# A macaron block on one core: ramp steps moved in front of GpSimd's tile work, and one more split on ScalarE

## The reference

```python
x = x + 0.5 * ffn(layernorm(x))      # 8 experts, one per token (argmax of the router), 128 -> 512 -> 128, relu
x = x + attn(layernorm(x))           # 16 heads of 8 channels, rms norm and rope on q and k, softmax
x = x + 0.5 * ffn(layernorm(x))      # the same weights again
```

```python
expert_idx = jnp.argmax(xf @ Wr.T + br, axis=-1)
h = relu(einsum('td,efd->etf', xf, W1) + b1[:, None, :])
y = einsum('etf,edf->etd', h, W2) + b2[:, None, :]
out = y[expert_idx, arange(tokens)]
```

## Time and profile before

| | us |
|---|---|
| three timed runs | 496.17, 498.18, 496.94 |
| their median | 496.94 |
| the profiled execution | 493.35 |
| its span, first to last instruction | 491.5 |
| busy in the span: PE, VectorE, ScalarE, GpSimd | 433.9, 380.5, 349.3, 358.6 |

### The profile page before, as it was taken

One profiled execution on the slowest core, in us unless ns is written; L12 is line 12 of the kernel. 1 busy time (PEld: TensorE's weight loads), 2 busy tenths in 40 slices (PEclk: granted clock), 3 DMA queues, 4 the chain that ended last, 5 costly groups with the idle time before them and its releaser, 6 DMA issues.

```text
span 491.5 us, 14012 instructions
## 1 busy us (share of the span) xinstructions
PE 433.9 (88%) x4108; PEld 322.8 (66%) x4108; DVE 380.5 (77%) x1037; ACT 349.3 (71%) x782; POOL 358.6 (73%) x579
## 2 busy tenths in 40 slices
PE   7998999969888989999999998988797979799994
PEld 4348998758665555656566655665464459789994
DVE  4785788758787788898988889888788647777772
ACT  4316776757745789999999898888666856557671
POOL 8028898999968588878684874399747616889985
PEclk9798999989997899999999999999899889999998
DMA  7962335251100000000000000000001123223210
GB/s 196 275 255 51 92 89 150 61 164 37 35 24 16 8 25 15 13 8 8 14 14 2 3 3 3 2 13 17 22 25 35 35 57 79 67 84 90 69 37 6
DMA packets 28649, 27.02 MB, mean 55 GB/s; under 512 B 5684, under 2 KB 25947, under 8 KB 28018
## 3 DMA queue, kind: packets, MB, share of 16 engines
q1 hardware_dynamic: 24034, 17.65, 12.1%
q0 software_dynamic: 4544, 8.49, 6.3%
HBM read 16.56 MB, written 12.71 MB: 60 GB/s over the span
## 4 chain that ended last, share of the span: by engine, by line
PE 39%; DVE 19%; POOL 18%; issue 13%; ACT 7%; DMA 1%; DVEq 1%; SPq 1%; ACTq 1%; POOLq 1%
DVE Smax L1732 8%; PE PS L1001 7%; PE PS L860 7%; PE PS L876 6%; PE PS L954 5%; POOL out L629 5%; PE PS L977 4%; POOL Unread L600 4%; PE PS L936 3%; DVE St L1375 2%; ACT Pt L1218 2%; PE PS L920 2%; POOL Pt L607 2%; POOL XX L638 1%; ACT QkT L1122 1%
## 5 line engine op out<-in xcount | busy, mean ns | idle before, releaser
L1732 DVE TENSOR_REDUCE Smax<-PS 128x4 f32<-128x1024 f32 x128 | 155.7, 1223 | 36.3 <-PE PS L954 35.5
L1218 ACT ACTIVATE Pt<-PS 128x1024 f32<-128x1024 f32 x128 | 126.4, 1024 | 20.2 <-PE PS L977 16.9
L876 PE MATMUL PS<-W,HsT 128*128 x624 | 87.4, 284 | 5.7 <-ACT HsT L1163 2.0
L860 PE MATMUL PS<-XsT,Ws 128*128 128x128 f32 x624 | 85.6, 282 | 2.4 <-ACT XsT L1122 2.0
L876 PEld LDWEIGHTS PS<-W,HsT 128*128 128x128 f32 x624 | 77.7, 196 | 10.5 <-issue 9.1
L860 PEld LDWEIGHTS PS<-XsT,Ws 128*128 128x128 f32 x624 | 79.0, 197 | 5.3 <-ACT XsT L1122 2.6
L1001 PE MATMUL PS<-Pt,Vg 128*32 128x256 f32 x1024 | 72.8, 404 | 0.2
L703 POOL TENSOR_TENSOR HL<-Rn,Zero 128x512 fp32r<-128x512 f32 x28 | 35.3, 1282 | 41.8 <-DVE Rn L1715 40.3
L954 PE MATMUL PS<-QkT 24*128 24x256 f32 x512 | 61.3, 312 | 3.0 <-DVE Smax L1732 2.0
L600 POOL MEMSET Unread<- 128x352 f32 (+1 forms) x140 | 62.0, 443 | 0.1
L607 POOL DMA_INDIRECT Pt<-rows,TokI x39 | 40.6, 1040 | 28.6 <-DVE TokI L1573 20.4
(11 more groups left out here) (251 smaller groups left out, 726.4 us busy)
## 6 DMA issues: line engine op xcount, KB each, us to landing
AtCol<-slots SPq DMA_DIRECT2D x39, 65.5 KB, 1.8
rows<-XX SPq DMA_DIRECT2D x8, 288.0 KB, 4.3
XX<-x SPq DMA_DIRECT2D x8, 256.0 KB, 5.1
W<-w1T SPq DMA_DIRECT2D x2, 1024.0 KB, 6.1
W<-w2T SPq DMA_DIRECT2D x2, 1024.0 KB, 9.3
mid<-mid_second SPq DMA_DIRECT2D x1, 1472.0 KB
mid<-Ys SPq DMA_DIRECT2D x16, 64.0 KB
QkT<-NmaxT SPq DMA_DIRECT2D x64, 4.0 KB
```

The source lines that it names most:

```text
L860: last = nc.tensor.matmul(PS[:, h_bank(n) + c // 2, (c % 2) * P:(c % 2 + 1) * P], Ws[:, n % R_WS, c * P:(c + 1) * P], XsT[:, n % 2, :], st ...
L876: last = nc.tensor.matmul(PS[:, y_bank(n), 0:P], HsT[:, n % 2, c, :], W2[:, ds(e * D_FF + c * P, P)], start=(c == 0), stop=(c == FC - 1))
L1218: nc.scalar.activation(Pt[:, m % 2, 2 * pair:2 * pair + 2, :, :].rearrange("p h c t -> p (h c t)"), PS[:, score_bank(m, pair):score_bank(m ...
L1732: nc.vector.tensor_reduce(Smax[:, b % 2, :, at:at + 33:32].rearrange("p t h -> p h t"), PS[:, max_bank(m, pair):max_bank(m, pair) + 2, :]. ...
```

## The change

In GpSimd's loop over the tiles the ramp steps of a tile go from behind its gathers and fetches to the head of the iteration, in front of the wait for `y_ready`. And `HIGH_TILE` gets a third entry: ScalarE writes the high part of sequence 2 at the end of tile 37; since `split` compares with `len(HIGH_TILE)`, GpSimd's `split(2)` then waits for `hi_ready` and does the low part only. ScalarE's `high` gets the wait for the transposes of the sequence two before, whose buffer it writes over.

```diff
-HIGH_TILE = {28: 0, 33: 1}
+HIGH_TILE = {28: 0, 33: 1, 37: 2}
...
             for t in range(S_TILES):
+                for n in RAMP_POOL.get(t, ()):
+                    step(n)
                 pool.wait_ge(y_ready, t + 1)
                 for _ in range(GATHERS.get(t, 1)):
                     if ahead:
...
                     fetch(j)
-                for n in RAMP_POOL.get(t, ()):
-                    step(n)
             stored(S_TILES)
...
             def high(b):
                 u, n = b % 2, SEQ_TILES * N_HEAD
                 act.wait_ge(rn_ready, b + 1)
+                if b >= 2:
+                    act.wait_ge(*qkT_turned(N_GRP * (b - 2) + N_GRP - 1))
```

## The result

The changed kernel is 1.1% slower; its median of 503.46 us lies outside the predicted range of 493.0 to 500.4.

What follows compares the result with a forecast made beforehand. It took GpSimd's queue order to bind from 73 to 107 us, then PE, ScalarE and VectorE in turn. Terms -0.3, +0.4, +0.35 and -0.25 gave +0.2 us: 497.1 us, range 493.0 to 500.4.

Steps and rivals of the forecast that it cites:

- The stall of normalise(0): VectorE's wait for the first sequence's second-half rope: rope(0, 1) 1.53 us earlier, so 4.64 us become 3.11.
- What takes it back: Tiles 25 to 35: gathers passed by the steps come later, leaving -0.3 us of the gain; bounds -1.53 and +0.6.
- The expected wait for gather 34: Tile 28: rope(1, 1) passes gather 34, which lands at 118.6 us, so scale(34) comes 0.5 us later.
- rope(3,0): Tile 36: the earlier rope slows VectorE's layernorm ahead of normalise(2); +0.4 us, bounds 0 and +2.2.
- no GpSimd wait before `rope(3, 0)`: Tile 36, sign that the forecast is right: GpSimd goes from fetch 15 to the rope without a wait.
- VectorE loses the whole of rope(3,0): Rival, layernorm of tile 36: delay 2.2 us instead of 0.4; 498.9 us, or 499.6 with one more instruction; chance 0.15.
- the clock at the start of attention: Rival, 153.5 to 163.8 us: clock holds, 493.5 us (chance 0.08), or falls in one more stretch, 500.7 (0.07).
- The Trainium skill's rule on the shared ports: VectorE beside GpSimd at tile 36: loser fully blocked; upper end if always VectorE, about +0.4 us if in turn.
- The high split: End of tile 37: two ScalarE activations, 1.16 us, make the XnT copy 0.35 us late; 1.16 uncovered, at best 0.
- The sum: Whole kernel: -0.3 + 0.4 + 0.35, less 0.25 for later VectorE loads, gives +0.2 us, 497.1 us timed.

Runs made afterwards that it cites:

- e1: Changed kernel without the third HIGH_TILE entry, so the early steps only and the high split left on GpSimd; ratio 1.0152 to the kernel before, median 504.76 us.
- e14: Whole change, but rope(3, 0) at the head of tile 35 and SyncE's second copy five tiles later; ratio 0.9990 to the kernel before, median 500.86 us.
- e3: Changed kernel with tile 36's step, rope(3, 0), put back behind the wait for y_ready; ratio 1.0069 to the kernel before, median 501.31 us.
- e5: Kernel before with only the steps of tiles 23 to 28 moved in front of the wait; ratio 1.0079, median 503.80 us.
- e13: Whole change, but rope(3, 0) at the head of tile 35 instead of tile 36; ratio 1.0071 to the kernel before, median 502.29 us.
- e11: Kernel before with the steps of tiles 23 to 28 in front and SyncE's second copy five tiles later; ratio 1.0068, median 497.10 us.
- e4: Kernel before with only tile 36's step, rope(3, 0), moved in front of the wait; ratio 1.0137, median 506.61 us.
- e7: Kernel before with seven unread VectorE products between the layernorm of tile 36 and normalise(2), no rope moved; ratio 1.0163, median 506.72 us.
- e8: Kernel before with tile 36's step in front of the wait and 18 unread products on PE where it waits; ratio 1.0084, median 502.44 us.

## Why the prediction was wrong

**The stall of normalise(0).** Right in kind: forecast 4.64 to 3.11 us, found 1.38. The old order gave 3.1 to 4.64 in its profiles, the early steps 1.38 in six and no wait in e1. It bought nothing: e14 has this gain without the losses and is level.

**What takes it back.** The place was right (`scale(31)`, with DMA named), and so was the account as far as it went: measured from the copy's issue gather 31 came as late as expected (`scale(31)` 7.2 us behind it, 7.3 before), and the whole saving of 3.26 us reappeared as one wait of 3.26 us. What it left out is a loss beyond the saving. The term was -0.3 with an upper bound of +0.6; e3, e5 and e13 show +0.7 to 0.8% by the ratios, 1.9 to 4.0 us by the medians. It goes with the copy (e14, e11); PE stood less than before (0.61 and 2.23 us against 3.87) and had 6.8 us at the lower clock in either profile, so its path stays open. The expected wait for gather 34 was hidden by this one and shows only where the copy is late (1.34 us in e14).

**rope(3,0): the step that failed.** The prediction has "I take +0.4 us: about half an instruction of 0.7". It failed twice, in size and in price. The layernorm grew by 2.48 - 0.92 = 1.56 us: four of its seven small instructions were lengthened, where I counted half of one rope instruction. (The sign "no GpSimd wait before `rope(3, 0)`" did not hold either: fetch 15 ahead of it waited 2.00 us for `output(35)`.) And the delay was then multiplied: this step alone costs 1.0137 (e4), some 6.8 us of 498. What I had as two rivals with separate chances, "VectorE loses the whole of rope(3,0)" (498.9 to 499.6) and "the clock at the start of attention" (500.7 for one stretch more), were here one mechanism: the first makes PE wait some 2 us ahead of the attention, and the second follows that wait (e7 gives both without the rope, e8 takes the second away). The price of the clock, by the estimate of a third of a us for each us more at 1.2 GHz (5.76 for 17), is some 5 us of the whole change's 5.4: its median time at that level is 53.5 us, against about 40 before. I had priced the delay at its own length, and left it out that it ends in a PE wait, though the earlier trace rows showed a PE wait with the lower clock right behind it.

The Trainium skill's rule on the shared ports (SBUF — State Buffer, section "SBUF: two separate sides") was weighed at its upper end, 2.2 us, and, with each engine the loser in turn, at about 0.4; the measured 1.56 lies between. Three of the small instructions ran in their usual 0.15 to 0.17 us beside the rope, four took 0.33 to 0.81.

**The high split.** Forecast +0.35, measured 1.0019 [0.9981, 1.0058]: agrees, and cannot be told from nothing.

**The sum.** 497.1 stood for +0.2 us. What came is +5.4 in the medians: two terms, one of 2 to 4 us where -0.3 stood and one of some 7 us, measured alone, where +0.4 stood. They do not add: e4 and e5 together would be 2.2%, the whole change is 1.1%, e1 1.5%. Why the whole is less than its parts is open; the meeting's effect on the clock is not the same each time (e1's profile has the meeting and PE's wait of 2.02 us, but only 3.4 us at the lower clock behind it and 3.4 more from 160.2 us, and none of its 6 runs has over 50 us; yet its ratio is 1.0152, which the clock does not explain).

## What to carry to other kernels

Price a delay on a helper engine by the TensorE wait that it ends in, and look at what the granted clock did behind waits of that length elsewhere in the same profile: here a delay of 2 us cost some 7. When a step is moved ahead of a wait, ask which event now releases it and which other engine works from the same event; two chains released together can meet in every run. And a wait that shows up on one engine is not yet a loss: e14's VectorE waits 4.8 us for gathers and loses nothing that can be measured. A stall that ends earlier moves the engines toward the next late transfer: look up what is in flight there before counting the saving.

## What the runs showed of the hardware

- PE's waits of 2.02, 2.22 and 2.72 us at this point (the changed kernel, e4, e7) were followed at once by 27.3, 27.3 and 30.7 us at a granted clock of 0.50, although PE was busy 25.18 of the 27.30 us in the first. Behind e1's 2.02 us came only 3.4.
- Behind waits of 0.26 to 1.15 us there (twelve profiles) the clock stayed at 1.00 for 8 us or more, except in e13 (3.4 us at 0.50 right behind it). Then, 8 to 11 us behind the wait, it fell in eleven of the twelve, for 3.4 to 17.1 us.
- Small VectorE instructions are lengthened beside GpSimd's indirect DMA too, not only beside its arithmetic: 0.72 us for one of 0.17, in e13 with fetch 15 alone beside it.
- A gather issued 0.8 us behind the large copy was there only 6.35 us later (106.45 to 112.80); with that copy moved away, within 3.1 us (e14).
